# Signals of TensorE's products: from a drain behind the last matmul instead of from the matmul

## What is computed

```python
def _L0_gnn_ref(X, edge_row, edge_col, edge_val, W, b):
    msgs = edge_val[:, None] * X[edge_col]
    h = jax.ops.segment_sum(msgs, edge_row, num_segments=N_NODES)
    return h @ W.T + b
...
# _L0_mix_ref
    q = jax.nn.elu(q) + 1.0
    k = jax.nn.elu(k) + 1.0
    kv = jnp.einsum('nshd,nshm->nhmd', k, v)
    ksum = jnp.sum(k, axis=1)
    z = 1.0 / (jnp.einsum('nlhd,nhd->nlh', q, ksum) + EPS_ATTN)
    t = jnp.einsum('nlhd,nhmd,nlh->nlhm', q, kv, z)
    x1 = layer_norm(t + x, ln1_g, ln1_b)
    h = jax.nn.gelu(jnp.einsum('nfc,oc->nfo', x1, W1) + b1, approximate=False)
    y = jnp.einsum('nfc,oc->nfo', h, W2) + b2
    return layer_norm(y + x1, ln2_g, ln2_b)
...
xn = _layernorm(x, axis=-1)
x = x + _L0_gnn_ref(xn, src, dst, edge_weight, ...) + _L0_mix_ref(xn[None], ...)[0]
x = x + _L0_ffn_ref(_layernorm(x, axis=-1)[None], ...)[0]
```

## Time and profile before

| what | us |
|---|---|
| three executions | 1011.49, 1011.53, 1013.69 |
| median | 1011.53 |
| span of the profiled execution, first to last instruction | 987.5 |
| median less span (start and end of the program, outside the profile's view) | 24.0 |
| TensorE busy in the span | 803.2 |

### The profile page before, as it was taken

One profiled execution on the slowest core, in us unless ns is written; L12 is line 12 of the kernel. 1 busy time (PEld: TensorE's weight loads), 2 busy tenths in 40 slices (PEclk: granted clock), 3 DMA queues, 4 the chain that ended last, 5 costly groups with the idle time before them and its releaser, 6 DMA issues.

```text
span 987.5 us, 14025 instructions
## 1 busy us (share of the span) xinstructions
PE 803.2 (81%) x4353; PEld 652.3 (66%) x4353; DVE 674.9 (68%) x1936; ACT 414.9 (42%) x1008; POOL 585.1 (59%) x648
## 2 busy tenths in 40 slices
PE   7879848888887688878874887778787787999997
PEld 6659746777766365555653665556665555999997
DVE  8889728899775453544554567666786677866676
ACT  3638734676572043233322232222332226766552
POOL 3947676788877666766665556656666500333353
PEclk9989988999889798999997879878898899999999
DMA  7210132233324323333333233324333611000000
GB/s 234 86 49 1 33 90 67 83 92 87 87 84 110 93 80 91 110 94 101 90 108 86 74 92 90 108 75 117 91 112 87 83 35 54 12 17 28 22 29 30
DMA packets 38993, 76.87 MB, mean 78 GB/s; under 512 B 9811, under 2 KB 22536, under 8 KB 38920
## 3 DMA queue, kind: packets, MB, share of 16 engines
q0 software_dynamic: 21120, 57.70, 21.4%
q1 hardware_dynamic: 17800, 18.29, 5.8%
HBM read 69.48 MB, written 6.48 MB: 77 GB/s over the span
## 4 chain that ended last, share of the span: by engine, by line
PE 34%; DVE 18%; issue 11%; another core or an unknown queue 7%; ACT 4%; DVEq 1%; POOLq 0%; POOL 0%; ACTq 0%
PE bank L2000 13%; DVE X L1281 8%; PE bank L1791 7%; PE bank L1842 4%; DVE ARENA L1269 2%; PE bank L1749 2%; PE bank L1849 2%; PE bank L1628 1%; PE bank L1916 1%; PE bank L1919 1%; DVE ST L1021 1%; PE bank L1857 1%; DVE KS L1330 1%; ACT OIA L816 1%
## 5 line engine op out<-in xcount | busy, mean ns | idle before, releaser
L699 POOL DMA_INDIRECT ARENA<-xg_rows,ARENA x440 | 427.4, 971 | 219.2 <-issue 118.4
L1281 DVE TENSOR_TENSOR X<-bank,X 128x256 f32 x440 | 185.2, 421 | 229.2 <-PE bank L1791 106.6
L1791 PE MATMUL bank<-ARENA 128*128 128x256 f32 x880 | 247.2, 422 | 57.6 <-DVE X L1281 43.8
L1791 PEld LDWEIGHTS bank<-ARENA 128*128 128x128 f32 x880 | 174.2, 209 | 108.8 <-DVE X L1281 52.9
L1269 DVE TENSOR_SCALAR ARENA<-iota,ARENA 128x128 f32<-128x128 f32 x440 | 150.3, 347 | 0.0
L1749 PE MATMUL bank<-OIA,ASA 128*128 128x128 f32 x676 | 98.5, 315 | 16.7 <-DVE ASA L1199 5.8
L1749 PEld LDWEIGHTS bank<-OIA,ASA 128*128 128x128 f32 x676 | 97.0, 231 | 20.5 <-issue 19.4
L816 ACT ACTIVATE OIA<-iota,LANE 128x128 f32<-128x128 f32 x286 | 85.9, 389 | 13.9 <-PE bank L1749 13.6
L984 ACT ACTIVATE HF<-bank,FB 128x262 f32<-128x262 f32 (+1 forms) x96 | 46.8, 487 | 40.8 <-DVE HFL L1566 20.5
L860 ACT ACTIVATE NK<-bank 128x256 f32<-128x256 f32 x25 | 9.6, 383 | 118.5 <-PE bank L1842 105.2
L2000 PE MATMUL bank<-QH,W1L 128*128 128x262 f32 (+1 forms) x192 | 55.2, 288 | 2.3 <-DVE W1L L1527 1.7
(11 more groups left out here) (317 smaller groups left out, 1564.6 us busy)
## 6 DMA issues: line engine op xcount, KB each, us to landing
ARENA<-xg_rows,ARENA POOLq DMA_INDIRECT x440
FW1A<-in_exp_w SPq DMA_DIRECT2D x8, 512.0 KB
xg_rows<-XGS SPq DMA_DIRECT2D x12, 256.0 KB, 2.1
out<-YO SPq DMA_DIRECT2D x24, 128.0 KB, 1.7
X<-in_x SPq DMA_DIRECT2D x1, 1664.0 KB, 12.4
X<-in_x SPq DMA_DIRECT2D x1, 1536.0 KB, 8.1
FW<-in_exp_w SPq DMA_DIRECT2D x2, 512.0 KB, 5.1
QKVW<-in_qkv_wT SPq DMA_DIRECT2D x1, 768.0 KB
```

Source lines behind the costliest of these rows:

```text
L699: pool.indirect_dma_start(RING[:, at, :], None, xg_dram, bass.IndirectOffsetOnAxis(ap=SIX[:, c:c + 1], axis=0)).then_inc(gathered[at // HA ...
L1281: V.tensor_tensor(xt, pair_bank(pair)[:, half * C:(half + 1) * C], xt, ALU.add).then_inc(x_added, 1)
L1791: ins = T.matmul(pair_bank(pair)[:, u * C:(u + 1) * C], SEL[:, t % 2 * HAND + k, :], RING[:, h * HAND + k, :], start=True, stop=True)
```

## The change

In stages 3 and 4, and for the pairs from number 66 on, the semaphore is no longer raised by the last matmul of a product. A drain stands behind it on TensorE's queue and raises it instead. A drain is an instruction of TensorE's sequencer that holds the sequencer until the instructions ahead of it are through. No matmul, no wait and no other engine's instruction is added, removed or moved. Stages 1, 2 and 5, `kv_summed`, and the pairs below number 66 keep the old signal.

```diff
+            def drained(signal):
+
+                pe.drain().then_inc(signal, 1)
...
                         ins = T.matmul(pair_bank(pair)[:, u * C:(u + 1) * C], SEL[:, t % 2 * HAND + k, :], RING[:, h * HAND + k, :],
                                        start=True, stop=True)
-                    ins.then_inc(chunk_mm[pair % 2], 1)
+                    if pair < PAIRS_A:
+                        ins.then_inc(chunk_mm[pair % 2], 1)
+                    else:
+                        drained(chunk_mm[pair % 2])
...
                 for s in slots:
-                    ins = transpose_tile(bank[0][:, s * C:(s + 1) * C], XN[:, tile(2 * i + s)])
-                ins.then_inc(a_tp, 1)
+                    transpose_tile(bank[0][:, s * C:(s + 1) * C], XN[:, tile(2 * i + s)])
+                drained(a_tp)
...
                     for c in range(CC):
-                        ins = T.matmul(bank[2 + s][:, :], XT[:, c, s, :], QKVW[:, c, C:3 * C], start=(c == 0), stop=(c == CC - 1))
-                    ins.then_inc(kv_done[s], 1)
+                        T.matmul(bank[2 + s][:, :], XT[:, c, s, :], QKVW[:, c, C:3 * C], start=(c == 0), stop=(c == CC - 1))
+                    drained(kv_done[s])
...
-                ins.then_inc(q_done, 1)
+                drained(q_done)
...
-                ins.then_inc(kvacc_done, 1)
+                drained(kvacc_done)
...
-                ins.then_inc(t_done, 1)
+                drained(t_done)
...
-                ins.then_inc(x1tp, 1)
+                drained(x1tp)
...
-                ins.then_inc(h_done, 1)
+                drained(h_done)
...
-                ins.then_inc(y_done, 1)
+                drained(y_done)
```

More of the change, by code:

```diff
@@ L1848, in a_project @@
                     for c in range(CC):
-                        ins = T.matmul(bank[5][:, h * 2 * P:h * 2 * P + n], QKVW[:, c, h * P:(h + 1) * P],
+                        T.matmul(bank[5][:, h * 2 * P:h * 2 * P + n], QKVW[:, c, h * P:(h + 1) * P],
                                        XT[:, c, 0:len(slots), :], start=(c == 0), stop=(c == CC - 1))
-                ins.then_inc(q_done, 1)
+                drained(q_done)
             def a_outer(i, slots, rows=P):
@@ L1856, in a_outer @@
                     for c in range(CC):
-                        ins = T.matmul(bank[4][:, c * VE:(c + 1) * VE], KS[0:rows, s, c * P:(c + 1) * P], VX[0:rows, s, c, :],
+                        T.matmul(bank[4][:, c * VE:(c + 1) * VE], KS[0:rows, s, c * P:(c + 1) * P], VX[0:rows, s, c, :],
                                        start=False, stop=False, skip_group_check=True)
-                ins.then_inc(kvacc_done, 1)
+                drained(kvacc_done)
             a_transpose(0, (0, 1))
@@ L1886, in b_attend @@
                     for c in range(CC):
-                        ins = T.matmul(bank[1 + s][:, c * VE:(c + 1) * VE], QT[:, c, toks(2 * i + s)], KVM[:, c, :], start=True, stop=True)
-                ins.then_inc(t_done, 1)
+                        T.matmul(bank[1 + s][:, c * VE:(c + 1) * VE], QT[:, c, toks(2 * i + s)], KVM[:, c, :], start=True, stop=True)
+                drained(t_done)
             def b_transpose(i, slots):
@@ L1894, in b_transpose @@
                 for s in slots:
-                    ins = transpose_tile(bank[0][:, s * C:(s + 1) * C], XS[:, s, :])
-                ins.then_inc(x1tp, 1)
+                    transpose_tile(bank[0][:, s * C:(s + 1) * C], XS[:, s, :])
+                drained(x1tp)
             def b_hidden(i, slots):
@@ L1904, in b_hidden @@
                     for c in range(CC):
-                        ins = T.matmul(bank[5][:, h * 2 * P:h * 2 * P + n], W1[:, c, h * P:(h + 1) * P],
+                        T.matmul(bank[5][:, h * 2 * P:h * 2 * P + n], W1[:, c, h * P:(h + 1) * P],
                                        XT[:, c, 0:len(slots), :], start=(c == 0), stop=(c == CC - 1))
-                ins.then_inc(h_done, 1)
+                drained(h_done)
             def b_project(i, slots):
@@ L1918, in b_project @@
                         T.matmul(bank[3 + s][:, c * P:(c + 1) * P], XT[:, c, s, :], ident[:, :], start=False, stop=False, skip_group_check=True)
-                    ins = T.matmul(bank[3 + s][:, 0:C], ones[0:1, :], B2R[0:1, :], start=False, stop=True)
-                ins.then_inc(y_done, 1)
+                    T.matmul(bank[3 + s][:, 0:C], ones[0:1, :], B2R[0:1, :], start=False, stop=True)
+                drained(y_done)
             pe.wait_ge(w12_in, 32)
```

## The result

| kernel | median us | lowest to highest | executions |
|---|---|---|---|
| before | 1011.51 | 1007.99 to 1013.69 | 4 |
| after | 1050.12 | 1044.87 to 1053.92 | 4 |

The change makes the kernel slower: the ratio is 1.038, with a 95% interval of 1.033 to 1.043. The prediction was 984 us and faster.

A forecast was written before the change was run, and what follows sets the result against it. It saw no engine full and blamed late TensorE signals. Keys and queries +7, between stages -5, mixing -30 sum to -28: 987.5 to 959.5 us of span, plus 24.0 around it, 983.5, say 984; range 955 to 1050.

The forecast's parts named there:

- so the results are not late, only the matmuls' updates: TensorE's products finish on time and only their semaphore updates come late, so a drain's signal would be prompt; 7 in 10.
- the first rival: The drain waits as long as the signal did, so nothing is won: about 1066 us (1035 to 1085), chance 0.23.
- main case: Drain signals prompt at 0.36 us each: 984 us, own range 955 to 1008, chance 0.53.
- What a drain costs: On TensorE when the next product is ready: 0.36 us per drain, bounds 0.26 and 0.56.
- Keys and queries: Seven drains on a step's path cost more than late signals: new step 15.28 us, +7 us in all.
- Between the stages: TensorE idles 7.52 us before its first `b_attend` row shown, with late pair signals ahead: -5 us taken.
- Mixing: Without late signals a step falls from 21.57 to 18.9 us: -29, with the end of the stage -30 us.
- The clock: TensorE's mean granted clock in mixing, 0.85 before, was to rise over 0.85 with less idle time.
- The base: The profile's span of 987.5 us, with 24.0 us taken to lie around it, making 1011.5.
- Second rival: Signals prompt but the drain dear, at the upper bound 0.56 us: 1026 us, chance 0.10.
- Third: Drain cheap at 0.26 us and POOL's gathers become the bound: about 969 us, chance 0.10.

The follow-up runs named there:

- a2: Kernel before with a drain behind `b_hidden` alone (13 drains): 1016.84 us, beside 1018.84 for before on the same chip.
- a1: The control: the kernel before, run again unchanged; 1015.90 us, beside 1018.84 for before on the same chip.
- b1: Changed kernel with the old signal behind all pairs, 116 drains left: 1014.39 us, ratio 1.016 to before.
- a3: Changed kernel with the old signal behind `b_hidden` alone, all other drains kept: 1034.34 us, beside 1018.84 for before.
- a5: Changed kernel with drains only in mixing and behind pairs from 129 on, keys and queries as before: 1027.66 us, ratio 1.029 to before.
- c1: Kernel before without the gathers of columns 132 to 439, so its output is another: 897.62 us, ratio 0.883 to before.
- d1_pause_two: Kernel before with two small POOL multiplications ahead of every fourth gather from column 132 on: 971.73 us, ratio 0.975.
- f2: Kernel before with two small POOL multiplications ahead of every fourth gather from column 132 on, run again on another chip: 971.56 us, ratio 0.976.
- e2_pause_drains: Changed kernel with two small POOL multiplications ahead of every fourth gather from column 132 on: 982.53 us, ratio 0.981 to before.

## Why the prediction was wrong

The step that failed is the one that the prediction said would decide: "so the results are not late, only the matmuls' updates". The runs show the other case. A drain behind `b_hidden` waits as long as the signal did (a2), so nothing is recovered, and the changed kernel is the first rival, "the drain waits as long as the signal did", which had 0.23 and stood at 1066 us (1035 to 1085). That 1050 is also the edge of the prediction's own range says nothing for its main case: the range took in the lower part of this rival. The argument from TensorE's rows was the mistake: that a matmul's row starts while signals are out does not show that the matmuls ahead are through, since the ends of these rows are modelled. The rival had the mechanism and not the sizes: it put 31 us on keys and queries (7 x 0.36 x 12 is 30) and 24 on mixing, and 12 and 29 were measured (9 and 29 against the control), since the holds that ended in the first stage paid back two thirds of the drains there.

The Trainium skill had this right where the prediction thought that the rows disagreed: "PSUM — Partial Sum Buffer", section "Engine vs sequencer instructions", says that an update attached to a matmul fires on its completion. The trace agrees with it: updates and drains are about equally late, 4.32 and 4.74 us in the mean behind `b_hidden` (a1, a2).

Point by point:

- *What a drain costs*, 0.36 us: right, 0.34 measured.
- *Keys and queries*, 15.28 us a step: nearly right, 15.66. Without gathers the path's drains cost 2.97 us against 2.52 + 0.10 in the sum. What was to be won there was won: only two short holds are left in this stage (0.9 and 0.2 us), and the clock rose to 0.99. The reading that the drains cost more than the late signals there was right. Why the holds went fits the run's length but was not tried by itself: the stream with drains is slower, and POOL's runs of gathers between 365 and 470 us are at most seven long, where before they were up to eleven.
- *Between the stages*, -5: not there. From the last full step's keys and values to the second `b_hidden` it is 56.6 us after, 56.4 before and 55.0 in the control.
- *Mixing*, 18.9 us a step: wrong in sign. Against the control's 23.22 the step grew by 2.6, eleven times 29 us. Without gathers the drains cost 17.99 - 16.69 = 1.3 of it. The other 1.3 come only with the holds. There a drain stops the stream, so that work which before was issued into the hold and came out in one burst is done after it, one piece at a time. In the step shown the first pair behind the hold takes 2.07 us, its add comes 2.25 us behind ScalarE (630.16; 0.16 in the control's step), and the granted clock from 627.9 to 632.4 us is 0.50. That this makes up the other 1.3 us is argued and not shown: a2 stops the stream as long behind `b_hidden` and loses nothing that shows. For it speak b1, where pairs with their old signal take the step down to 23.18 (on a chip where before was faster), and a3, which takes it down in part. How much of it is the lower clock (0.79, in the control 0.81) can't be separated: TensorE's idle stretches and its half clock come together.
- *The clock* over 0.85 in mixing: wrong, 0.79.
- *The base*: 24.0 us around the span was wrong, it is 1.7. The rows were of an execution 2% shorter than the median, and the loss of 60 us between the two profiles holds 22 that the change has nothing to do with. The table ahead of the prediction said that the profile gives no total beside the span. This error did not decide the sign.
- *Second rival*, the drain dear: ruled out by the 0.34. *Third*, gathers as the bound: true only once next to nothing is held; with the pauses 20.8 us a step are near POOL's own 20.5.

Without its false premise the sum would have been: 12 x 1.0 in keys and queries (2.97 paid, 2.0 won back by holds that end), nothing between the stages, and in mixing 11 x 1.3 for the drains themselves, +26 us, and on top the share of the standing stream, which no row of before could give.

## What to carry to other kernels

- When a consumer starts late after a matmul's row has ended, find out first whether the completion is late or only its signal: one drain at one place, read in the profile, tells it. A recorded end of a matmul is a model; behind `b_hidden` the drain's end stood up to 6.4 us behind it (a2), and ScalarE started with the drain's end.
- A drain on TensorE's queue cost 0.34 us here where the next product was ready, and it turns each late completion into a stop of the whole stream. Put none behind products that the engine could run past.
- Where many gathers follow one another on GpSimd, look for late completions from the fifth on, and try a short pause. Here 77 pauses of under 1 us gave 2.5%, on an engine that had the time to spare, and took time where it had not.

## What was not expected of the hardware

- Matmuls that touch nothing of the gathers, such as `b_hidden`, completed up to 6.4 us late while GpSimd issued indirect gathers back to back, 1.25 us apart; in the two steps shown the hold ended 3.0 us behind the start of the run's last gather (624.84 to 627.88, 622.44 to 625.45), about 0.6 us after its last packet (2.42 us behind its start). In a2 ten of the eleven late drains ended 3.0 to 3.2 us behind that start; but over the late drains of after, a2, a3, a5 and b1 it is 0.1 to 4.4 us, so this is no fixed time. Signals of the other engines stayed prompt: of the updates in the control's trace from 333 to 800 us, all 350 of VectorE's and all 95 of ScalarE's came within 0.02 us of an instruction's end, while 69 of TensorE's 221 came over 0.15 us behind the last end that can have raised them. Without gathers (c1) none of TensorE's 339 did. The Trainium skill says in "SBUF — State Buffer", section "Who interferes with whom", that PE never waits on anyone. That is about ports of SBUF; as a rule on when a product is complete, the runs here speak against it.
- With runs of up to four gathers and 2.1 us from the fourth to the fifth nothing is "remote" in d1_pause_two and f2, but not every hold is gone in each kernel: in e2_pause_drains 9 of 270 drains still ended 0.17 to 1.33 us late. The single pauses of about half a microsecond released `b_hidden` in every step but not the pairs.
- Open: by what path a run of gathers holds a completion on TensorE. Each time here was taken with the profiler's records being written, so whether the holds are there without it is open too; from 333 to 800 us the trace of before has an update for 372 of 535 of VectorE's instructions that raise one, that of c1 for all 729. No run took the gathers off GpSimd.
- The executions of before spread from 991 to 1028 us over all chips, and by up to 2.9% on one; those with two multiplications ahead of each fourth gather from 968.6 to 974.8 over two chips. That the holds make the spread fits the 2.00 and 4.32 us of `HS` wait in an execution of 989 and one of 1014 us, but was not tried further.
